# Delta attention with its values projected once, convolved by VectorE and turned, and its small products redistributed

## What is computed

```python
mixed = jnp.einsum('bth,ch->btc', hidden_states, qkv_w)
x = lax.conv_general_dilated(mixed.transpose(0, 2, 1), conv_w, window_strides=(1,),
        padding=[(KCONV - 1, 0)], feature_group_count=CONV_DIM, ...)      # 4 taps per channel
z = jnp.einsum('bth,vh->btv', hidden_states, z_w)
q, k, v = jnp.split(x.transpose(0, 2, 1), 3, axis=-1)
beta = jax.nn.sigmoid(bb)
alpha = jnp.exp(-jnp.exp(A_log) * jax.nn.softplus(aa + dt_bias))          # = exp(g)
def step(S, inp):                                                         # over the tokens
    S = S * alpha_t[..., None, None]
    kv = jnp.einsum('bhk,bhkv->bhv', k_t, S)
    S = S + jnp.einsum('bhk,bhv->bhkv', k_t, (v_t - kv) * beta_t[..., None])
    return (S, jnp.einsum('bhk,bhkv->bhv', q_t, S))
o = o * lax.rsqrt(jnp.mean(jnp.square(o), axis=-1, keepdims=True) + EPS) * norm_w
o = o * (z * jax.nn.sigmoid(z))
out = jnp.einsum('btv,hv->bth', o.reshape(b_, t_, VAL_DIM), out_w)
```

## Time and profile before

| | us |
|---|---|
| median of three runs | 8056.37 |
| the profiled execution | 8045.66 |
| its span on the core | 8043.8 |
| stage `a1s` (from 1018.0 to 2584.4) | 1566.4 |
| PE / DVE / ACT / POOL busy in that stage | 1472.8 / 1384.1 / 782.1 / 473.4 |

### The profile page before, as it was taken

One profiled execution on the slowest core, in us unless ns is written; L12 is line 12 of the kernel. 1 busy time (PEld: TensorE's weight loads), 2 busy tenths in 40 slices (PEclk: granted clock), 3 DMA queues, 4 the chain that ended last, 5 costly groups with the idle time before them and its releaser, 6 DMA issues. The chain is left out here.

```text
span 8043.8 us, 271416 instructions
## 1 busy us (share of the span) xinstructions
PE 6799.7 (85%) x118712; PEld 4816.6 (60%) x118712; DVE 5751.5 (72%) x10171; ACT 3577.8 (44%) x6436; POOL 2800.7 (35%) x1921
## 2 busy tenths in 40 slices
PE   7999789999998898898998998998997798445566
PEld 3444478888886566666665665665664555345434
DVE  6666379999997786786885885885886577842366
ACT  3555245555554565564664664664664222210121
POOL 0110023332332673673773773773772000011000
PEclk8999599999999999999999999999998899555557
DMA  0000000000000321221221221221220000000000
GB/s 15 1 1 1 2 6 5 4 4 4 4 3 10 78 73 48 69 75 44 73 74 43 73 75 42 76 75 42 76 76 17 16 1 2 2 3 4 5 0 14
DMA packets 187953, 249.14 MB, mean 31 GB/s; under 512 B 58998, under 2 KB 85493, under 8 KB 185845
## 3 DMA queue, kind: packets, MB, share of 16 engines
q1 hardware_dynamic: 186740, 231.40, 11.0%
HBM read 27.84 MB, written 2.10 MB: 4 GB/s over the span
## 5 line engine op out<-in xcount | busy, mean ns | idle before, releaser
L1702 POOL TENSOR_TENSOR XNT<-XNT 128x1024 f32<-128x1024 f32 x384 | 907.0, 2362 | 317.9 <-DVE XNT L1871 312.8
L1773 PE MATMUL wa_front<-w_wqkv,wa_xT 128*128 128x512 f32 x1920 | 941.4, 614 | 30.0 <-ACT wa_qT L1766 11.1
L1705 POOL TENSOR_TENSOR XNT<-XNT,wa_rnorm 128x1024 f32<-128x1024 f32 x320 | 608.7, 1902 | 256.6 <-ACT wa_rnorm L1728 232.2
L1773 PEld LDWEIGHTS wa_front<-w_wqkv,wa_xT 128*128 128x128 f32 x1920 | 334.7, 194 | 296.6 <-issue 256.7
L1868 DVE TENSOR_TENSOR XNT<-wa_front,w_scaled 128x1024 f32<-128x1024 f32 x320 | 390.3, 1220 | 159.4 <-PE wa_front L1773 159.4
L447 PE MATMUL a0h_ring<-a0h_QT,a0h_KT 32*128 32x512 f32 (+3 forms) x1536 | 443.8, 549 | 14.4 <-ACT a0h_E L565 10.4
L565 ACT ACTIVATE a0h_E<-a0h_ring 128x512 f32<-128x512 f32 (+1 forms) x640 | 320.5, 555 | 279.9 <-PE a0h_ring L447 278.6
L1871 DVE TENSOR_TENSOR XNT<-wa_front,w_scaled 128x512 f32<-128x512 f32 x640 | 409.2, 681 | 0.0
L1878 DVE TENSOR_REDUCE wa_least<-wa_sq 128x16 f32<-128x1024 f32 x320 | 380.0, 1187 | 14.6 <-ACT wa_sq L1720 12.6
L1720 ACT ACTIVATE wa_sq<-wa_front 128x1024 f32<-128x1024 f32 x320 | 326.0, 1020 | 133.4 <-PE wa_front L1773 105.2
L1779 PEld LDWEIGHTS wa_front<-consts,XNT 128*128 128x128 f32 x2560 | 277.9, 142 | 158.4 <-POOL XNT L1705 109.5
(11 more groups left out here) (621 smaller groups left out, 17523.9 us busy)
## 6 DMA issues: line engine op xcount, KB each, us to landing
wa_v_look<-wa_v_all SPq DMA_DIRECT2D x960, 128.0 KB, 2.4
wa_v_look<-wa_v_all SPq DMA_DIRECT2D x640, 64.0 KB, 2.1
wal_v_look<-wal_v_all SPq DMA_DIRECT2D x192, 128.0 KB, 2.4
wal_v_look<-wal_v_all SPq DMA_DIRECT2D x128, 64.0 KB, 2.1
w_wqkv<-in_L_ffn_Wqkv_dram SPq DMA_DIRECT2D x6, 1024.0 KB, 6.4
w_wo<-in_L_ffn_Wo_dram SPq DMA_DIRECT2D x6, 512.0 KB, 6.9
w_wqkv<-in_L_ffn_Wqkv_dram SPq DMA_DIRECT2D x12, 256.0 KB, 7.7
f2w_raw<-in_L_ffn_w_dram SPq DMA_DIRECT2D x48, 64.0 KB, 1.9
```

Of the source, the lines that this page charges most:

```text
L1702: g.tensor_tensor(rot[:, at], rot[:, at], part[:, at], ALU.add).then_inc(s[summed], 1)
L1705: g.tensor_tensor(rot[:, at], rot[:, at], spread(rnorm[:, at, :], HDW), ALU.mult).then_inc(s[done], 1)
L1773: last = pe.matmul(front[:, first + i, :], x_of(which), wqkv[:, (2 * n + i) * 512:(2 * n + i + 1) * 512], start=True, stop=True)
```

## The change

The change touches this stage alone. It does seven things.

- Values: the four scaled weight matrices and their sixteen products go. In their place stand one 512-column product (`raw_values`), a third copy to `hist` by ACT (`keep_raw(2, 0)`), a third convolution by DVE into `vconv` (`convolve(VC, ...)`), and, in the next step, four transposes by PE (`turn_values`).
- `xs` and its copy by POOL go; the projections read the normalized input directly.
- The decay sums, four products of 128 columns with `ga` as weights, become one product of 512 columns with `ga` streamed; `ga` is made from `c.upto` and not from `c.after`.
- POOL makes the five levels in one instruction of 640 columns, and makes `sb` ahead of them.
- The four DVE copies of `place` become one POOL multiplication with a block mask (`c.head_blocks`), 512 columns, behind the fifth `X_ready`.
- `rstd` is no longer multiplied into `y`; it scales the output where this is added to `X`: four scalar_tensor_tensor of 128 columns for one tensor_tensor of 512.
- The product for `z` moves on PE from behind `tx(5)` to ahead of `tx(4)`, and POOL's shift of `hist` waits for `vconv_ready` too.

```diff
-                def vtok_part(b):
+                def raw_values():
+                    if j is None:
+                        return
+                    pe.wait_ge(s["raw_copied"], 3 * j + 1)
+                    pe.matmul(flat(bank[0][:]), weights(j)[:, V_W, :], x_of(j), start=True, stop=True).then_inc(s["raw_ps"], 1)
+
+                def turn_values():
                     if q is None:
                         return
-                    if b == 0:
-                        pe.wait_ge(s["ktok_ready"], q + 1)
-                        if j is not None:
-                            pe.wait_ge(s["raw_copied"], 2 * j + 2)
-                    for n in range(TAPS):
-                        last = pe.matmul(bank[3][:, b, :], xs[:, q % 2, b, n:n + P], weights(q)[:, V_W + n, :], start=(n == 0),
-                                         stop=(n == TAPS - 1))
-                    if b == G - 1:
-                        last.then_inc(s["vtok_ps"], 1)
+                    pe.wait_ge(s["ktok_ready"], q + 1)
+                    pe.wait_ge(s["vconv_ready"], q + 1)
+                    if j is not None:
+                        pe.wait_ge(s["raw_copied"], 3 * j + 2)
+                    turn_four(bank[3], vconv[:, q % 2], s["vtok_ps"])
...
-                    four_of(bank[7], lambda b: ga[:, b, :], lambda b: c.upto, s["dt_ps"])
+                    pe.matmul(flat(bank[7][:]), c.after, flat(ga[:]), start=True, stop=True).then_inc(s["dt_ps"], 1)
                 zt(3)
-                vtok_part(0)
+                raw_values()
                 tx(3)
-                vtok_part(1)
+                turn_values()
                 zt(4)
-                vtok_part(2)
+                if q is not None:
+                    if r is not None:
+                        pe.wait_ge(s["o_done"], r + 1)
+                    four_of(bank[5], lambda b: x_of(q)[:, b, :], lambda b: weights(q)[:, Z_W, :], s["z_ps"])
                 tx(4)
-                vtok_part(3)
...
                 evict_z(4)
+                keep_raw(2, 0)
...
-                    g.tensor_tensor(lev[:, 0], Nc[:], small[:, 0:1, :].broadcast_to(tiny), ALU.mult).then_inc(s["lev0_ready"], 1)
-                    g.tensor_tensor(lev[:, 1:SMALL], Nc[:].unsqueeze(1).broadcast_to([P, SMALL - 1, G, 32]),
-                                    small[:, 1:SMALL, :].unsqueeze(2).broadcast_to([P, SMALL - 1, G, 32]),
+                    g.tensor_tensor(lev[:], Nc[:].unsqueeze(1).broadcast_to([P, SMALL, G, 32]),
+                                    small[:, 0:SMALL, :].unsqueeze(2).broadcast_to([P, SMALL, G, 32]),
                                     ALU.mult).then_inc(s["lev_ready"], 1)
+                    g.wait_ge(s["X_ready"], LD * (q + 1))
+                    g.tensor_tensor(XT[:, q % 2].rearrange("p b (k x) -> p b k x", x=32),
+                                    XTc[:].unsqueeze(2).broadcast_to([P, G, 4, 32]),
+                                    c.head_blocks.rearrange("p (k x) -> p k x", x=32).unsqueeze(1).broadcast_to([P, G, 4, 32]),
+                                    ALU.mult).then_inc(s["x4_ready"], 1)
...
                         g.wait_ge(s["conv_ready"], 2 * j + 2)
+                        g.wait_ge(s["vconv_ready"], j + 1)
...
-                    v.tensor_tensor(mine, bank[4][:], mine, ALU.add).then_inc(s["added"], 1)
+                    for b in range(G):
+                        last = v.scalar_tensor_tensor(out=mine[:, b], in0=bank[4][:, b, :], scalar=rstd[:, b:b + 1],
+                                                      in1=mine[:, b], op0=ALU.mult, op1=ALU.add)
+                    last.then_inc(s["added"], 1)
...
                 grow(4)
-                if q is not None:
-                    place()
                 convolve(1, 2, T0)
+                convolve(VC, 0, 0)
...
                     v.tensor_copy(XT[0:64, slot, :, 64:P], bank[4][0:64, :, 0:64]).then_inc(s["x6_ready"], 1)
+                convolve(VC, 0, T0, False)
                 if r is not None:
                     v.wait_ge(s["std_ready"], r + 1)
-                    chain(v.reciprocal(rstd[:], std[:]))
-                    v.tensor_tensor(y[:], y[:], spread(rstd[:], P), ALU.mult).then_inc(s["y_ready"], 1)
+                    v.reciprocal(rstd[:], std[:]).then_inc(s["rstd_ready"], 1)
```

More of the change, by code:

```diff
@@ L1013, in turn_weights @@
                     pe.wait_ge(s["w_ready"], 2 * n + 1)
-                    pe.wait_ge(s["scaled"], n + 1)
                     if n >= 1:
                         pe.wait_ge(s["T64b_ready"], step)
-                for k, m in enumerate((0, 1, 3, 4) if part == 0 else (2, 5, 6, 7)):
+                for k, m in enumerate((0, 1, 3, 4) if part == 0 else (2,)):
                     last = pe.transpose(bank[2][:, k, :], raw_w[:, m, :], c.ident)
@@ L1143, in _ @@
                         pe.wait_ge(s["N_ready"], q + 1)
[L1144 removed]
+                    pe.matmul(flat(bank[0][:]), weights(j)[:, K_W, :], x_of(j), start=True,
                               stop=True).then_inc(s["raw_ps"], 1)
@@ L1212, in keep_weights @@
                     a.wait_ge(s["loaded"], 8 * 16 * (n + 1))
-                    if n >= 1:
-                        a.wait_ge(s["w_ps"], 2 * n)
-                    for i in reversed(range(TAPS)):
-                        last = a.activation(raw_w[:, 2 if i == 0 else 4 + i, :], raw_w[:, 2, :], ACT.Copy,
-                                            scale=taps[:, n % 2, 2, i:i + 1])
-                    last.then_inc(s["scaled"], 1)
                 a.wait_ge(s["w_ps"], 2 * n + 1 + part)
@@ L1225, in keep_weights @@
                 else:
-                    a.activation(into[:, V_W:V_W + TAPS, :], bank[2][:], ACT.Copy).then_inc(s["w_ready"], 1)
+                    a.activation(into[:, V_W, :], bank[2][:, 0, :], ACT.Copy).then_inc(s["w_ready"], 1)
             keep_weights(0, 0)
@@ L1363, in _, with convolve @@
                     decay = [spread(of_chunk(decays[:, n], r), P) for n in range(2)]
-                def convolve(n, first, end):
+                def convolve(n, first, end, begin=True):
                     if j is None:
                         return
-                    into = conv[:, j % 3, n]
-                    t = taps[:, j // BLOCKS % 2, 1 - n]
-                    if first == 0:
-                        v.wait_ge(s["raw_copied"], 2 * j + n + 1)
+                    into = vconv[:, j % 2] if n == VC else conv[:, j % 3, n]
+                    t = taps[:, j // BLOCKS % 2, 2 if n == VC else 1 - n]
+                    if first == 0 and begin:
+                        v.wait_ge(s["raw_copied"], 3 * j + n + 1)
                         chain(v.tensor_scalar(into, hist[:, n, :, T0:], t[:, T0:TAPS], None, ALU.mult))
@@ L1388, in grow @@
                     v.transpose(flat(T[:]), flat(XTc[:])).then_inc(s["T_ready"], 1)
-                def place():
-                    for k in range(4):
-                        last = v.tensor_copy(XT[quarter(k), slot, :, quarter(k)], XTc[quarter(k)])
-                    last.then_inc(s["x4_ready"], 1)
                 if q is not None:
@@ L1406, in _ @@
                         v.wait_ge(s["dt_ps"], j)
-                    v.tensor_tensor(ga[:], c.after.unsqueeze(1).broadcast_to(four),
+                    v.tensor_tensor(ga[:], c.upto.unsqueeze(1).broadcast_to(four),
                                     spread(of_chunk(g_all[:], j), P),
```

66 lines of the change are left out of this document (29 added, 37 removed).

## The result

| | before | after |
|---|---|---|
| median, us (4 runs each, same chip) | 8063.31 | 8141.80 |
| range, us | 8049.25 to 8074.13 | 8133.03 to 8159.64 |
| ratio, with its 95% interval | | 1.0101 (1.0076 to 1.0126) |
| profiled execution / its span | 8045.66 / 8043.8 | 8159.64 / 8157.9 |
| start of one `N` to the next | 23.93 | 25.34 |

The account below looks back on a forecast made before the run. DVE and POOL, excluding each other on SBUF reads, were taken to set the step: 1.1 - 0.1 + 0.35 to 0.5, finer walk 1.45 us, times 63, with end corrections 92 us. Predicted 8145 us, range 8045 to 8195.

Parts of the forecast that it names:

- The rule: A DVE instruction reading two SBUF tensors and a POOL instruction exclude each other; the later waits, and they take turns.
- `N` to `grow(1)`: First part of a step: `R`, levels, `ga` and `XTc` wait in turn behind `sb`; +1.1 us with the scaled output.
- if `R` wins against `sb`: Bound on the first part of a step: `sb` waits instead and `ga` behind it, +0.25 us.
- `grow(1)` to `grow(4)`: Middle of a step: same DVE instructions while POOL rests, unchanged less 0.1 us for PE's moved work.
- `grow(4)` to `N`: End of a step: convolution, masking, `Estrict`, `Eincl` and value instructions collide; 8.10 us becomes 8.45, +0.35 to 0.5.
- the chain of turns: Behind `grow(4)`: masking, convolution's last instruction, `Estrict`, values' tensor_scalar wait in turn; later the first value instruction meets `Eincl`.
- The sum: Whole step: 1.1 - 0.1 + 0.35 to 0.5 gives +1.35 to 1.5 us, 1.45 by the finer walk.
- three idle spans of VectorE: In one step before the change: DVE idles 0.39, 0.45 and 0.35 us behind PE and POOL, otherwise runs on.
- idle ahead of `zt(1)`: Sign in the profile after: PE shows idle spans, above all there, busy some 20.3 of 25.4 us.
- rival (c): Whole stage: the granted clock falls from 1.00, products lengthen, further collisions cost 0.5 to 1.0 us each; above 8195, chance 0.06.
- Rival (a): Both halves of a step: the collisions do not fall so; +0.3 us a step, +19 us, 8075; chance 0.15.
- Rival (b): Whole step: DVE's sum decides and gets faster, -1.3 us a step, -84 us, 7972; chance 0.17.

Follow-up runs that it names:

- both edits: Changed kernel with `sb` behind the levels, waiting for the first `XTc`, and the values' first convolution tap on ScalarE: 8047.73 us, 0.9989.
- the unread product: 384-column TensorE product, result unread, ahead of `zt(5)`: 0.9964 on both edits with `ga` and `Eincl` on GpSimd, 0.9969 on both edits, 1.0089 on the changed kernel.

## Why the prediction was right

- *The rule.* The first step of the kernel before had shown the convolution beside GpSimd, and the steady steps now show the same lengths: 1.62 and 1.48 against the 1.63 and 1.50 of the earlier trace rows. Holding `sb` back gave 0.68 of the 1.41 us back with all the work kept; the first tap on ScalarE brought it to 1.31, but that took work off VectorE as well. So for the first half the cause is shown by experiment; for the second half it rests on the lengths and ends of the rows. That the effect comes from a port shared by the two engines is the reading of it in the Trainium skill (SBUF — State Buffer, "Who interferes with whom"); the runs show exclusion and turns, not the port.
- *`N` to `grow(1)`*, +1.1 forecast: 8.35 and 8.24 in two steps that follow each other, against 7.18, mean +1.1. The step of the earlier trace rows was a long one there; by the means it is 8.32 against 7.06, +1.25. The size was about right, but the order that was walked held in less than half of the steps. I had put "if `R` wins against `sb`" among the bounds, at +0.25; it wins in 36 of 64, by 0.02 in the first step shown, and costs about 0.1 (8.35 against 8.24), because the levels then do the waiting. The walk had `newS` start 0.15 behind `N`; it starts at 0.30 (1502.01), and `sb` with it later, so `R` is first in most steps in which `kS` does not come late from TensorE. That the two orders are about equally long was luck. Within the term, `T` came 5.1 to 5.2 behind `N` (forecast 5.0), and the scaled output added 0.3 from `T` to `grow(1)` (3.16 against 2.85), where 0.45 was booked.
- *`grow(1)` to `grow(4)`*, -0.1: 8.53 (1518.59 - 1510.06) against 8.65 (23.93 - 7.18 - 8.10); by the means 8.54 against 8.76, -0.2.
- *`grow(4)` to `N`*, 8.45 forecast: 8.60 and 8.41, and by the means 8.47 against 8.09. The step with 8.41 is the usual one (the median is 8.41), and there the chain of turns ran as walked, up to the first value instruction that waits for `Eincl`: the three take 2.63 (start 1499.08). In the step with 8.60 the last copy to `XT` waited for TensorE (0.42) at the lower clock; the three then start behind the end of `Eincl` and take 2.31, so that the wait costs only 0.2.
- *The sum.* By the means it is 1.25 - 0.22 + 0.38 = 1.41, where 1.45 was forecast: the first term came out larger and the second smaller, and the two misses nearly cancel. The forecast change of the program was 89 us (8145 against 8056.37), the measured one 78.5; that the time itself was met within 4 us is partly because the kernel before came out 7 us slower in this comparison.
- *Idle time before.* The prediction counted three idle spans of VectorE. There is a fourth, of 0.40 us, ahead of `gatez` (at 1515.48, waiting for ScalarE, 64 times in the stage). No term hangs on it: after the change `gatez` comes later and does not wait.
- *TensorE*: idle ahead of `zt(1)` as forecast, 0.97 us in a step. It was busy 22.0 us a step (1214.94 / 1400 x 25.34), where some 20.3 was put, since the dips lengthen its work. The clock at 1.00 was an assumption, rival (c) its denial. The clock did fall, but in a kernel in which VectorE and its turns decide this cost little: `kS` and the last copy wait for TensorE 14.5 us over 1100 to 2500, 0.26 a step, and raising the clock moved these waits elsewhere. Rival (c) had its mechanism half right and its price wrong.
- *Rival (a)*, no collisions, is out by the lengths. *Rival (b)*, VectorE's sum of -1.3 us, is out: even with both edits the step is 0.10 above that of the kernel before, not 1.3 below it. The wait behind the levels (1.44) and the convolution's own turn (1.62 at 1509.46 in that run) remain there, which neither edit removed.

What was not settled is what brings the clock's dips; and whether an order on GpSimd exists with no collision at all was not tried. The fastest versions are about equal: 0.9964 with `ga` and `Eincl` moved and the unread product, 0.9969 with both edits and that product, and 0.9971 with all but the values; each is some 25 us faster than the kernel before, and their intervals overlap.

## What to carry to other kernels

An instruction that is short by itself is not cheap where the other engine has one in flight that excludes it (here `ga` went from 0.69 us to 1.54 or 2.03, and the tensor_scalar from 0.45 to 1.48). Before moving two-input VectorE work, list the starts and ends of both engines in one column and walk the turns; a rare place in the old trace (here the first chunk) may show the price. Where two instructions are released by the same event, a new order is not enough: one has to wait for the other's end (25.45 with the new order, 24.66 with the wait).

## What was not expected of the hardware

- In the rows shown, VectorE and GpSimd take strict turns while both have an instruction pending, and a start 0.02 us earlier is enough to go first: `R` 0.69 and `sb` 1.58. In the other order, with `sb` ahead, it is `sb` 1.04 and `R` 1.12.
- TensorE's granted clock dipped in this stage with the engine busy 1214.94 of 1400 us; the dip shown follows an idle span of 0.87 us. Before, with 1337.48 busy, it was 1.00. In the kernel with both edits, busy 1217.65, it was 0.98; so the busy sum alone does not order the kernels.
